# A second layer's pipeline re-cut: five stages in place of six, part of a scan moved into its own batch's round, and small products in pairs

## The reference

```python
xa = _ln(x, ln1_w, ln1_b)
sx = jnp.concatenate([state[:, 1:2] - xa[:, :1], xa[:, :-1] - xa[:, 1:]], axis=1)
xxx = jnp.tanh((xa + sx * maa_x) @ maa_w1).reshape(b, l, 5, DM)
xxx = jnp.einsum('blfd,fde->blfe', xxx, maa_w2)
xm = xa[:, :, None] + sx[:, :, None] * (maa_stack + xxx)
xk, xw, xv, xr, xg = (xm[:, :, j] for j in range(5))
w = jnp.exp(-jnp.exp(time_decay + jnp.tanh(xw @ td_w1) @ td_w2)).reshape(b, l, h, s_)
# r, k, v: xr, xk, xv times a 512 x 512 matrix each; g: silu of xg's product
def step(s, rkvw):                      # over the 256 positions, 32 heads of 16
    a = k_t[..., :, None] * v_t[..., None, :]
    out = jnp.einsum('bhi,bhij->bhj', r_t, u * a + s)
    s = a + w_t[..., :, None] * s
x1 = x + group_norm(out) * g @ Wo.T     # then the channel part:
rr = jax.nn.sigmoid(xr2 @ Wfr.T)        # xr2, xk2: mixes of _ln(x1) with its shift
kk = jnp.square(jax.nn.relu(xk2 @ Wfk.T))
return x1 + rr * (kk @ Wfv.T)
```

## Time and profile before

| | |
|---|---|
| timed runs | 2166.06, 2168.41, 2172.05 us; median 2168.41 |
| the profiled execution's own time | 2155.11 us |
| its span, first to last instruction | 2153.4 us |
| instructions | 28651 |
| TensorE busy | 1940.0 us, 90% |
| VectorE busy | 1437.3 us, 67% |
| ScalarE, GpSimd busy | 867.1 us, 523.9 us |

### The profile page before, as it was taken

How to read it: one execution, slowest core, us unless ns; L and a number is a source line. 1 busy time by engine, 2 the same in 40 slices (tenths; PEclk the granted TensorE clock), 3 DMA queues, 4 the chain that set the end, 5 groups by cost and what they waited for, 6 DMA issues and landing times.

```text
span 2153.4 us, 28651 instructions
## 1 busy us (share of the span) xinstructions
PE 1940.0 (90%) x11012; PEld 1334.3 (62%) x11012; DVE 1437.3 (67%) x2431; ACT 867.1 (40%) x2024; POOL 523.9 (24%) x245
## 2 busy tenths in 40 slices
PE   5789999999999997999998999999999997885456
PEld 4566666666666664676775767757667656563233
DVE  3366667666666542122778787878878878999942
ACT  2466666666666743222312423414224213130221
POOL 1233334333343321020302202204104023130100
PEclk9799999999999998999999999999999998897687
DMA  7000010000001113544538437446365453443221
GB/s 207 25 1 25 11 35 21 16 25 11 26 14 71 40 64 98 203 139 153 188 113 271 150 125 253 148 147 219 115 191 191 137 197 108 156 137 119 90 78 49
DMA packets 155215, 234.90 MB, mean 109 GB/s; under 512 B 24152, under 2 KB 72024, under 8 KB 155080
## 3 DMA queue, kind: packets, MB, share of 16 engines
q1 hardware_dynamic: 138184, 216.28, 30.3%
q10 hardware_dynamic: 16896, 16.80, 2.3%
HBM read 191.09 MB, written 41.96 MB: 108 GB/s over the span
## 4 chain that ended last, share of the span: by engine, by line
PE 42%; DVE 7%; DMA 3%; ACT 2%; issue 2%; POOL 2%; SPq 1%; POOLq 0%; DVEq 0%; ACTq 0%
PE b_f_bank L1747 9%; PE b_a_bank L1770 9%; PE b_f_bank L1737 7%; PE b_c_bank L1780 6%; PE b_a_bank L1789 4%; DVE b_ring L1982 3%; PE b_c_bank L1770 3%; DMA b_o<-b_o_all 2%; PE b_y_bank L1809 2%; DVE b_ring L1971 1%; PE b_c_bank L1789 1%; PE b_f_bank L1897 1%; POOL b_mixed L1656 1%; DVE b_ring L1989 1%; DMA k_w_early<-in_w_dram 1%
## 5 line engine op out<-in xcount | busy, mean ns | idle before, releaser
L401 POOL TENSOR_TENSOR a_prob<-a_prob,a_rowinv 128x1024 f32<-128x1024 f32 x128 | 242.2, 1893 | 507.8 <-DVE a_rowinv L854 507.8
L1982 DVE TENSOR_TENSOR_SCAN b_ring<-b_ws,b_ring 128x1028 f32<-128x1028 f32 x128 | 354.0, 2806 | 6.1 <-ACT b_ring L2194 3.2
L1086 ACT ACTIVATE a_prob<-a_score,a_low 128x256 f32<-128x256 f32 x512 | 253.6, 497 | 226.5 <-DVE a_low L846 226.5
L1656 POOL TENSOR_TENSOR b_mixed<-b_mixed,b_xaT 128x1024 f32<-128x1024 f32 x40 | 119.9, 2998 | 606.6 <-DVE b_mixed L1999 606.5
L1747 PE MATMUL b_f_bank<-k_w_early 128*128 128x512 f32 x448 | 204.1, 603 | 12.3 <-DMA k_w_early<-in_w_dram 8.1
L1737 PE MATMUL b_f_bank<-k_hT_early,k_w_early 128*128 128x256 f32 x896 | 205.0, 385 | 6.5 <-ACT b_xaT L2174 5.7
L846 DVE CUSTOM_DVE_ANT_0 a_score<-a_score,a_fill 128x256 f32<-128x256 f32 x512 | 196.6, 447 | 4.8 <-DVE a_score L833 0.3
L1737 PEld LDWEIGHTS b_f_bank<-k_hT_early,k_w_early 128*128 128x128 f32 x896 | 169.3, 192 | 36.0 <-issue 14.0
L833 DVE SCALAR_TENSOR_TENSOR a_score<-a_S,a_mask 128x1024 f32<-128x1024 f32 x128 | 150.7, 1219 | 48.2 <-PE a_S L595 48.2
L1770 PE MATMUL b_a_bank<-b_mixed,b_shared 128*128 128x256 f32 x768 | 172.7, 382 | 4.4 <-POOL b_mixed L1656 3.2
L826 DVE TENSOR_SCALAR a_ctxT<-a_O,a_vec 128x256 f32<-128x256 f32 x64 | 31.0, 484 | 208.7 <-PE a_O L625 208.7
(11 more groups left out here) (162 smaller groups left out, 3053.1 us busy)
## 6 DMA issues: line engine op xcount, KB each, us to landing
k_w_early<-in_w_dram SPq DMA_DIRECT2D x64, 1024.0 KB, 5.3
b_vs<-b_v_all SPq DMA_DIRECT2D x32, 512.0 KB, 6.1
b_shared<-in_Wv_dram SPq DMA_DIRECT2D x8, 1024.0 KB, 5.5
b_shared<-in_Wk_dram SPq DMA_DIRECT2D x8, 1024.0 KB, 6.0
b_shared<-in_Wg_dram SPq DMA_DIRECT2D x8, 1024.0 KB, 7.5
b_shared<-in_Wo_dram SPq DMA_DIRECT2D x8, 1024.0 KB, 10.3
b_shared<-in_Wfv_dram SPq DMA_DIRECT2D x8, 1024.0 KB, 6.6
b_shared<-in_Wfk_dram SPq DMA_DIRECT2D x8, 1024.0 KB, 5.6
```

The source lines that it names most:

```text
L401: nc.gpsimd.tensor_tensor(two, two, inv.to_broadcast([P, 2 * TT, SEQ]), ALU.mult)\
L1086: last = nc.scalar.activation(prob[:, slot, a * SEQ:(a + 1) * SEQ], score[:, j, a * SEQ:(a + 1) * SEQ], ACT.Exp, bias=low[:, head, a:a + 1 ...
L1656: nc.gpsimd.tensor_tensor(mixed[:, f % 2, :, :], mixed[:, f % 2, :, :], xaT[:, :, 1:SEQ + 1], ALU.add)\
L1982: last = nc.vector.tensor_tensor_scan(x_, flat(ws[:, :, :]), x_, 0.0, ALU.mult, ALU.add)
```

## The change

- Stages n and a become one, so that a batch's layer norm, mixes, projections and its steps 0 to 2 of the scan stand in one round. The stage s takes steps 3 to 7 in the next round and then, in the same round, all up to xcT, sx2 and the mixes of the channel part. The last stage d has kk, rr, kv and the output. `STAGES = "lfasd"`; `pipeline` itself is unchanged and runs ten rounds, i = 2 to 11.
- Mixes 0 and 1, and 2 and 3, are issued by turns (`mix_pair`), in two halves each; mix4 and td2 are issued by turns over two halves of the rows (`by_halves`), for which their weights are loaded twice, to both halves of the rows. t1's weights get the columns of mix 4 a second time.
- xaT and t1 move from the "f" banks to the "a" banks.
- The four stores of k, w, v, r get a semaphore each, and SyncE loads ks and ws as soon as their own store is done.
- Three of the four memsets before the first loads go, and there are four more small loads of weights.

TensorE's order in a full round becomes: ff1(0), kk, xaT, add_rows(s, 2), rr, t1, add_rows(s, 3), mixes 0 and 1 first half, kv, their second half, ff1(1), add_rows(s, 4), ff1(2), k, td1, mixes 2 and 3 first half, ff1(3), add_rows(s, 5), ff2(0), their second half, td2, ff2(1), add_rows(s, 6), ff1(4), v, add_rows(s, 7), r, mix4, dev, ff1(5), var, g, bonus, ff2(2), add_rows(a, 0), wo, ff2(3), ff1(6), add_rows(a, 1), xcT, ff1(7), ff2(4), ff2(5), hT3, ff2(6), ff2(7).

VectorE's: layer norm, step(s, 3), z, step(s, 4), shifts 0 and 1, first half, kv's gate, second half, output, step(s, 5), step(s, 6), shifts 2 and 3, first half, f2(0), second half, step(s, 7), f2(1), l's norm, shift 4, rk, step(a, 0), the gate product gT, bonus, yg, f2(2), step(a, 1), wo's sum with its layer norm, f2(3), step(a, 2), f2(4), the channel mixes, f2(5) to f2(7).

The core of the diff (a line of three dots marks what is left out):

```diff
-            "a": [("mix0", "dve")] * 2 + [("mix1", "dve")] * 2
-            + [("k", "act")] * 2 + [("mix2", "dve")] * 2 + [("td1", "act")] + [("td2", "act")] * 2
-            + [("v", "act")] * 2 + [("mix3", "dve")] * 2 + [("r", "act")] * 2 + [("mix4", "dve")] * 2
+            "a": [("xaT", "act")] * 2 + [("t1", "act")] + [("mix0", "dve"), ("mix1", "dve")] * 2
+            + [("k", "act")] * 2 + [("td1", "act")] + [("mix2", "dve"), ("mix3", "dve")] * 2 + [("td2", "act")] * 2
+            + [("v", "act")] * 2 + [("r", "act")] * 2 + [("mix4", "dve")] * 2
             + [("g", "dve")] * 2 + [("bonus", "dve")] * 2 + [None],
             "c": [("dev", "act")] * 2 + [("var", "act")] * 2 + [("wo", "dve")] * 2 + [("xcT", "act")] * 2
-            + [("rr", "act")] * 2 + [("kk", "act")] * 2 + [("kv", "dve")] * 2,
+            + [("kk", "act")] * 2 + [("rr", "act")] * 2 + [("kv", "dve")] * 2,
         }
...
-        F1, F2 = ("f", "f1", "act"), ("f", "f2", "dve")
-        XAT, T1, HT3 = ("n", "xaT", "act"), ("n", "t1", "act"), ("l", "hT3", "act")
-        F_TILES = [F1, F1, F1, F1, F2, F2, XAT, XAT, F1, F1, T1, F2, F2, F1, F1, F2, F2, HT3, HT3, F2, F2]
+        F1, F2, HT3 = ("f", "f1", "act"), ("f", "f2", "dve"), ("l", "hT3", "act")
+        F_TILES = [F1, F1, F1, F1, F2, F2, F1, F1, F2, F2, F1, F1, F2, F2, HT3, HT3, F2, F2]
...
-        STAGES = "lfnasc"
+        STAGES = "lfasd"
...
-        kwvr_out = Tally(sem("kwvr_out"), 4, 16, by="act")
+        kwvr_out = {n: Tally(sem(n + "_out"), 1, 16, by="act") for n in "kwvr"}
...
+            def store_scan(s):
+
+                sp.wait_ge(osum_made.sem, osum_made.at(s, 2))
+                alone(sp)
+                by_tile = o_dram[s, :, :].rearrange("(h u j) (e t) -> j e h u t", h=N_HEADS, j=JCOLS, e=2)
+                for m in range(JMOD):
+                    sp.dma_start(by_tile[m // 2, m % 2, :, :, :], osum[m * N_HEADS:(m + 1) * N_HEADS, :, :])\
+                        .then_inc(o_out.sem, 16)
...
+                if s is not None:
+                    store_scan(s)
                 if a is not None:
                     load_shared("Wg", (a, "v", 1))
...
+                if s is not None:
+                    sp.wait_ge(o_out.sem, o_out.at(s, 1))
+                    alone(sp)
+                    sp.dma_start(o[:, :, :], o_dram[s, :, :].rearrange("(c p) t -> p c t", p=P)).then_inc(o_in.sem, 16)
...
+                if a is not None:
+                    sp.wait_ge(kwvr_out["v"].sem, kwvr_out["v"].at(a, 1))
+                    alone(sp)
+                    load_part(a, 0)
+                    load_part(a, 1)
+                    sp.wait_ge(kwvr_out["r"].sem, kwvr_out["r"].at(a, 1))
+                    alone(sp)
+                    sp.wait_ge(weighed.sem, weighed.at(a, 0))
+                    alone(sp)
+                    load_rows(a, rs, r_dram, r_in)
...
+            def mix_pair(a, fs, k):
+
+                if fs[0] == 0 and k == 0:
                     pe.wait_ge(*emptied(a, "t1", 0))
+                for f in fs:
+                    pe.wait_ge(*bank_free(a, f"mix{f}", k))
+                for m in range(2):
+                    c = 2 * k + m
+                    for f in fs:
+                        rows = slice(f * MIX_RANK, (f + 1) * MIX_RANK)
+                        last = nc.tensor.matmul(tile(f"mix{f}", k)[:, m * SEQ:(m + 1) * SEQ],
+                                                maa_w2[rows, 0, c * P:(c + 1) * P], t1[rows, 0, :], start=True, stop=True)
+                        if m == 1:
+                            last.then_inc(full_sem(f"mix{f}"), 1)
+
+            def by_halves(b, name, rank, weight_of, act_of):
+
+                for k in range(2):
+                    pe.wait_ge(*bank_free(b, name, k))
+                for m in range(2):
+                    for k in range(2):
+                        rows = slice(k * rank, (k + 1) * rank)
+                        last = nc.tensor.matmul(tile(name, k)[:, m * SEQ:(m + 1) * SEQ], weight_of(rows, 2 * k + m),
+                                                act_of(rows), start=True, stop=True)
+                        if m == 1:
+                            last.then_inc(full_sem(name), 1)
...
+                    step(a, 0)
...
+                if s is not None:
+                    dve.wait_ge(yn_made.sem, yn_made.at(s, 1))
...
+                if a is not None:
+                    step(a, 1)
...
+                if a is not None:
+                    step(a, 2)
```

More of the change, by code:

```diff
@@ L1313, in tile @@
                 return BANKS["f"][place[name][k] % 2]
-            which, n = first[name]
-            return BANKS[which][(n + k) % len(BANKS[which])]
+            which, n = where[name][k]
+            return BANKS[which][n % len(BANKS[which])]
         def upto(which, n, who):
@@ L1326, in filled @@
                 return f_full[st].sem, f_full[st].at(b, f_upto(n, st))
-            which, n = first[name]
-            return full[which].sem, full[which].at(b, upto(which, n + k, None))
+            which, n = where[name][k]
+            return full[which].sem, full[which].at(b, upto(which, n, None))
         def emptied(b, name, k):
@@ L1351, in full_sem @@
                 return f_full[F_TILES[place[name][0]][0]].sem
-            return full[first[name][0]].sem
+            return full[where[name][0][0]].sem
         def empty_sem(name):
@@ L1357, in empty_sem @@
                 return f_taken[st, who].sem
-            which, n = first[name]
+            which, n = where[name][0]
             return taken[which][TILES[which][n][1]].sem
@@ L1889, in body @@
[L1889 to L1900 removed]
+                    pe.wait_ge(rk_made.sem, rk_made.at(a, 1))
@@ new lines, in body @@
+                if a is not None:
+                    shift_pair(a, (0, 1), 1)
+                if d is not None:
+                    dve.wait_ge(*emptied(d, "kv", 1))
+                    x_ = xr[:, :, :].rearrange("p a n -> p (a n)")
+                    nc.vector.scalar_tensor_tensor(out=x_, in0=flat(o[:, :, :]), scalar=0.5, in1=x_, op0=ALU.mult,
+                                                   op1=ALU.add).then_inc(out_made.sem, 1)
+                if s is not None:
+                    step(s, 5)
+                    step(s, 6)
@@ new lines, in body @@
+                if a is not None:
+                    for k in range(2):
+                        shift(a, 4, k)
+                    dve.wait_ge(*emptied(a, "r", 1))
+                    nc.vector.tensor_tensor(mixed[:, 1, :, :], kT[:, :, :], rT[:, :, :], ALU.mult).then_inc(rk_made.sem, 1)
+                    step(a, 0)
+                    for k in range(2):
+                        dve.wait_ge(tanh_g.sem, tanh_g.at(a, k + 1))
+                        x_ = flat(gT[:, 2 * k:2 * k + 2, :])
+                        nc.vector.scalar_tensor_tensor(out=x_, in0=x_, scalar=1.0, in1=tile("g", k)[:, :],
+                                                       op0=ALU.add, op1=ALU.mult).then_inc(empty_sem("g"), 1)
+                    for k in range(2):
+                        dve.wait_ge(*filled(a, "bonus", k))
+                        nc.vector.tensor_tensor(flat(mixed[:, 0, 2 * k:2 * k + 2, :]), tile("bonus", k)[:, :],
+                                                flat(vT[:, 2 * k:2 * k + 2, :]), ALU.mult)\
+                            .then_inc(empty_sem("bonus"), 1)
@@ new lines, in body @@
+                if s is not None:
+                    for k in range(TT):
+                        dve.wait_ge(*filled(s, "wo", k))
+                        nc.vector.tensor_tensor(xr[:, k, :], tile("wo", k)[:, :], xr[:, k, :], ALU.add)\
+                            .then_inc(empty_sem("wo"), 1)
+                    dve.wait_ge(*emptied(s, "wo", 1))
+                    ln_stats(s, 1, xr, c_links, c_var)
+                    h2 = flat(sq[:, :, :]).rearrange("p (a n) -> p a n", a=TT)
+                    ln_apply(s, 1, xr, h2, c_links, c_std, c_h)
```

653 lines of the change are left out of this document (289 added, 364 removed).

## The result

| | kernel before | changed kernel |
|---|---|---|
| median, us | 2165.99 (18 runs, 2161.79 to 2173.96) | 2172.36 (18 runs, 2167.35 to 2176.02) |
| profiled execution, own time, us | 2155.11 | 2168.41 |
| its span, us | 2153.4 | 2166.7 |
| its second layer, us | 1293.7 | 1303.5 |

The changed kernel is slower by a little: the ratio of times is 1.0023, 95% interval 1.0014 to 1.0033, some 5 us. The forecast was +19 us and 2187. The profile of the kernel before, which the forecast was built on, shows an execution that was faster than each of the 18 timed ones.

A forecast was written before the change was run, and what follows sets the result against it. TensorE was taken to bound full rounds (145.4 of 148.2 us). Pairs save 5.0 per round, but waits make it 155; ten rounds sum to 1313 against 1293.7, and +19 on the 2168.41 median gives 2187, range 2127 to 2225.

The forecast's parts named there:

- Part 1: Paired mixes, td2 included, on TensorE: blocks from 1.99 to 1.15 us, minus 5.0 us per batch, full-round work 140.4.
- Part 2: One batch's chain in a full round: no wait at t1, 1.5 us lost at td2's banks.
- Part 3: Scan result out and back in one round: dev waits 7.1 us, slow clock adds 2.0, late VectorE 3.3; round 155.
- i = 3 and i = 8: Second-layer rounds without channel part and without l respectively: 151 us each.
- the last of the sum: Final step: the second layer's +19 us is added to the median of 2168.41, giving 2187.
- i = 2: Second-layer round with l, f and a: 119 us, with TensorE work about 101.
- i = 9: Round with a, s and d, without feed-forward: 133 us with latencies.
- the last two: Rounds i = 10 and 11: 139 us together, ending in the old last round's 83.5.
- B: Rival, chance 0.30: wait for the scan's result mostly covered, so faster, 2145 or 2133; decides under 151 per full round.
- C: Rival, chance 0.13: halfway, full rounds of 151 to 153, time unchanged at 2168 give or take 6.
- A: Main case, chance 0.45: the serial store and load make it slower, 2187, own range 2160 to 2215.
- D: Rival, chance 0.12: engine overlap or a late z lengthens the scan side to 160 per round, giving 2217.

The follow-up runs named there:

- no_trip: Changed kernel with o loaded together with bv and g, from the stored v instead of the stored scan: 2128.01 us, ratio 0.9821 to the kernel before.
- fill_take: Changed kernel with ff1(5) and ff2(2) ahead of dev and VectorE's addition of ff2(5) ahead of the channel mixes: 2127.51 us, ratio 0.9815.
- same_rows: Changed kernel with all eight matmuls of each mix block reading one row group: 2209.87 us, ratio 1.0197 to the kernel before.
- fill: Changed kernel with the tiles ff1(5) and ff2(2) moved ahead of dev on TensorE: 2141.01 us, ratio 0.9874 to the kernel before.
- early_take: Changed kernel with VectorE's addition of ff2(5) moved ahead of the eight channel mixes: 2153.17 us, ratio 0.9940 to the kernel before.
- Experiments 4 and 11: Changed kernel and kernel before rerun unaltered: 2173.68 and 2168.86 us; kernel before with o loaded from stored v ahead of the store's wait: 2166.56 us.
- no_pairs: Changed kernel with only the matmul order inside pairs and halves turned back: 2171.77 us, ratio 1.0013 to the kernel before.
- before_again: Kernel before, unaltered, run once more for a second profile: 2168.86 us.
- before_halves: Kernel before with only td2 and mix4 done by halves on weights loaded twice: 2161.15 us, ratio 0.9967.
- vs_first: Changed kernel with the two loads of vs issued on SyncE's queue ahead of the wait for the stored scan: 2199.47 us, ratio 1.0153.

## Why the prediction was right in direction and wrong in size

**Right, with their sizes.** Part 1: blocks of 1.13 for 1.15, TensorE's work of a full round 140.4 forecast and 140.6 to 141.0 where no gap slows it (no_trip, fill_take); same_rows shows that it hangs on the two row groups. Part 2: t1 without a wait in full rounds, td2 1.1 for 1.5. Part 3: dev waits for o for 6.2 (7.1 forecast; o landed after 6.4, not 7.3), VectorE stands for 3.8 ahead of step (a, 0) (5 forecast), the hidden rows' second bank comes 2.6 late (3.3), the clock costs 3.4 (144.0 less 140.6) where 2.0 was entered, since the second gap slows its tiles too. Together 153.5 for the 155 of the sum. no_trip, fill and early_take each take one of these terms away and give back what the steps say. i = 3 and i = 8 came out within 0.2 us of the 151 forecast.

**The failed step is the last of the sum**: "0.6% under the median ... I add the 19 us to the median". The +19 is a difference against one execution of the kernel before whose full rounds of 147.2 to 148.2 were taken as its steady length. Experiments 4 and 11 show rounds of 148.2, 150.5 and 152.2 in the same kernel, and a second layer of 1305.5 instead of 1293.7. The first layer of that execution, 859.7, is the shortest of all fourteen profiles too; the others have 861.6 to 864.6, whichever kernel they are of. The changed kernel's full rounds stay within 153.1 to 153.9 in both its profiles. Against the second profile of the kernel before, which lies near the median, its second layer is longer by 3.3 us (1308.8 against 1305.5) and not by 9.8 or 19. Adding a difference from a lucky execution to the median counted 11 us of luck as a loss (2165.99 less 2155.11), and the median of three runs that it was added to was 2.4 too high. The absolute sum would have come out nearer: 859.7 for the first layer, 1313, and 1.7 around the span make 2174.4, against a median of 2172.36. That closeness is in part luck as well, since its second layer is too long (9.5 us, and 4 by the second profile) and its first too short (3.5).

**Terms of the sum that were mis-sized**, from the windows after: i = 2 took 122.9 for 119; the four full rounds 614.0 for 620; i = 9 131.5 for 133; the last two 133.2 for 139, since from the end of the last row sum on they took 77.3 us and not the old 83.5. In all 9.5 us too long (4 in the second profile). So the layer is +9.8 in the two first profiles, not +19; with 3.5 us more in the first layer the spans differ by 13.3; and the two executions lay 10.9 and 4.0 us under their medians, which leaves 6.4, the difference of the medians.

**The rivals.** B named 151 us for a full round as the point from which it decides. Full rounds stayed at 153.5, and the versions that get under 151 (early_take 150.1, fill 148.5, no_trip 147.6, fill_take 146.0) are faster than before by 0.6, 1.3, 1.8 and 1.9%: the mechanism is the one described, and the wait decides it. The time that came is C's, 2168 give or take 6, but by A's rounds and not by C's 151 to 153: the level was off, not the rounds. A's own range, 2160 to 2215, holds it as well. D did not occur.

## What to carry to other kernels

When a store and a load of one batch move into the same round, count how much ready work stands between the producer and the reader on the bounding engine; the trip was 14 us here, the cover 8, and moving two tiles in front of the reader turned a change of +5 us into one of -26.7, and with one addition moved on VectorE into -39.5. On a queue with a load that someone waits for, that load goes first: two transfers ahead of it cost 27 us here, and 37 in the best version, where they were meant to start another engine earlier. And a difference worked out against a profiled execution is to be added to that execution's own time; how far its rounds repeat has to be asked before it is added to a median.

## What the runs showed of the hardware

- Matmuls on two row groups overlap whatever their order inside a block of eight: 1.14 us for four and four in a row (no_pairs), 1.13 alternating, 1.99 in one group (same_rows). The block on 64 rows each does the same: 1.13, 1.14 and 1.96.
- A gap can cost more than its own length, by the clock behind it. In the changed kernel dev took 3.78 us after a wait of 6.2 (granted clock 0.50), 1.99 without one in no_trip (1.00); a gap of 2.6 us made the 7.03 us of two tiles 8.47 (0.83), while after 0.42 they took 7.10. In fill a gap of 1.27 left var at 1.97, against 1.89 without. The length of the gap alone does not decide: behind a wait of 2.1 us for v the clock fell in one round of before_again and not in the next, and in before_halves it fell behind one of 0.76.
- A load of 512 KB landed in 6.4 us behind the stores and one weight load, and in 9.2 with two broadcast loads of the same size issued just ahead of it (vs_first).
